# Attention values: one eviction into a plain buffer and four DMAs onto the block diagonal, in place of four evictions

## The reference

```
x = _ln(transpose(msa, (0, 3, 2, 1)), ln_m_g, ln_m_b)      # 256 columns of 32 tokens of 64
q = heads(x @ Wq);  k = heads(x @ Wk);  v = heads(x @ Wv)  # 8 heads of 8
g = sigmoid(heads(x @ Wg + bg))
scores = einsum('blhnd,blhmd->blhnm', q, k) / sqrt_c + bias
w = softmax(scores, axis=-1)
attn = g * einsum('blhnm,blhmd->blhnd', w, v)
out = attn @ Wo + bo
...
logits = x @ router_w + router_b                           # 2048 tokens, 8 experts, the best 2 each
h = silu(gate) * up
y = einsum('te,etd->td', weights, expert_out)
```

## Time and profile before

| what | us |
|---|---|
| median of 3 runs | 355.83 |
| the runs | 355.47 to 358.65 |
| the profiled execution, its own time | 359.83 |
| its span in the trace | 358.0 |
| busy in the span: TensorE | 295.7 (83%) |
| VectorE | 276.0 (77%) |
| ScalarE | 209.9 (59%) |
| GpSimd | 202.7 (57%) |

### The profile page before, as it was taken

One profiled execution on the slowest core, in us unless ns is written; L12 is line 12 of the kernel. 1 busy time (PEld: TensorE's weight loads), 2 busy tenths in 40 slices (PEclk: granted clock), 3 DMA queues, 4 the chain that ended last, 5 costly groups with the idle time before them and its releaser, 6 DMA issues.

```text
span 358.0 us, 11098 instructions
## 1 busy us (share of the span) xinstructions
PE 295.7 (83%) x3773; PEld 178.3 (50%) x3774; DVE 276.0 (77%) x569; ACT 209.9 (59%) x380; POOL 202.7 (57%) x176
## 2 busy tenths in 40 slices
PE   0596868878878755977989989999999999899970
PEld 0186435545545532322446556666666666566640
DVE  3998785989999996778658767888888878688750
ACT  0277688989999964277135435555555555455520
POOL 2833132786889889452233476575756575565451
PEclk9998975989999997885599999999999999999995
DMA  7450100355544457679126777977768687767942
GB/s 183 84 180 3 61 2 6 117 187 171 185 168 142 152 168 226 234 221 240 37 53 112 114 124 123 134 127 125 132 119 134 116 149 109 128 120 131 116 63 30
DMA packets 70656, 45.00 MB, mean 126 GB/s; under 512 B 47992, under 2 KB 63608, under 8 KB 70240
## 3 DMA queue, kind: packets, MB, share of 16 engines
q1 hardware_dynamic: 62368, 34.09, 37.4%
q0 software_dynamic: 7488, 10.39, 20.3%
q10 hardware_dynamic: 768, 0.14, 0.3%
HBM read 23.43 MB, written 9.63 MB: 92 GB/s over the span
## 4 chain that ended last, share of the span: by engine, by line
PE 41%; DVE 16%; DMA 13%; issue 11%; ACT 9%; POOL 4%; POOLq 2%; ACTq 0%; DVEq 0%
PE bank L862 15%; DMA out_dram<-w_stage,gate 8%; PE bank L885 7%; DMA w_stage<-token_rows,gate 4%; ACT kq L1040 3%; PE bank L679 3%; DVE maxes L1327 3%; PE bank L762 2%; PE bank L588 2%; PE bank L850 2%; PE bank L670 2%; DVE s_exp L1336 2%; POOLq L527 2%; PE bank L552 2%; DMA w_exp<-in_L_conv_pairs_dram 1%
## 5 line engine op out<-in xcount | busy, mean ns | idle before, releaser
L862 PE MATMUL bank<-w_exp,v_t 128*128 x468 | 113.6, 379 | 2.0 <-DVE v_t L1526 1.4
L534 POOL DMA_INDIRECT out_dram<-w_stage,gate x39 | 62.2, 1594 | 54.4 <-DMA out_dram<-w_stage,gate 32.5
L862 PEld LDWEIGHTS bank<-w_exp,v_t 128*128 128x128 f16 x468 | 45.9, 98 | 42.2 <-issue 4.2
L885 PE MATMUL bank<-w_exp,kq 128*128 x468 | 57.9, 273 | 1.0 <-DVE w_stage L1572 0.8
L520 POOL DMA_INDIRECT w_stage<-token_rows,gate x39 | 40.1, 1029 | 27.9 <-ACT gate L1131 11.2
L1152 ACT ACTIVATE kq<-w_stage 128x512 f16<-128x512 f32 x38 | 23.9, 630 | 53.8 <-DVE w_stage L1555 53.8
L885 PEld LDWEIGHTS bank<-w_exp,kq 128*128 128x128 f16 x468 | 45.6, 98 | 15.0 <-issue 1.1
L438 POOL TENSOR_TENSOR w_exp<-w_stage,w_exp 128x1024 f16<-128x1024 f32 x16 | 34.1, 2134 | 12.3 <-ACT w_exp L1051 12.3
L1562 DVE TENSOR_TENSOR kq<-w_stage,kq 128x512 f16<-128x512 f32 x38 | 26.3, 693 | 16.7 <-ACT kq L1152 16.7
L1547 DVE TENSOR_TENSOR kq<-bank,v_t 128x512 f32<-128x512 f32 x39 | 26.9, 691 | 11.4 <-PE bank L862 11.3
L1555 DVE TENSOR_TENSOR w_stage<-s_exp,kq 128x512 f32<-128x512 f32 x39 | 27.1, 694 | 3.9 <-DVE kq L1547 0.4
(11 more groups left out here) (255 smaller groups left out, 519.2 us busy)
## 6 DMA issues: line engine op xcount, KB each, us to landing
w_stage<-in_L_ffn_gate_w_dram SPq DMA_DIRECT2D x8, 512.0 KB, 3.6
w_stage<-in_L_ffn_up_w_dram SPq DMA_DIRECT2D x8, 512.0 KB, 3.4
w_stage<-in_L_ffn_down_w_dram SPq DMA_DIRECT2D x8, 512.0 KB, 3.6
x_rows<-in_x_dram SPq DMA_DIRECT2D x8, 256.0 KB, 5.9
out_dram<-x_rows SPq DMA_DIRECT2D x4, 512.0 KB, 6.1
v_t<-in_L_ffn_up_b_dram SPq DMA_DIRECT2D x2, 1024.0 KB, 10.6
token_rows<-z_stack SPq DMA_DIRECT2D x4, 512.0 KB, 6.4
z_two<-z_stack SPq DMA_DIRECT2D x6, 256.0 KB, 2.4
```

Of the source, the lines that this page charges most:

```text
L534: pool.indirect_dma_start(out, bass.IndirectOffsetOnAxis(t_scatter[:, b:b + 1], 0), yw[b % 2], None, compute_op=ALU.add).then_inc(s[f"y_la ...
L862: mm = pe.matmul(GU[par][k][:], xs[par][:, c, :], w_exp[:, w * W_EXP + k * W_PIECE + c * FF:][:, bass.ds(e, FF)], start=(n == 0), stop=(n ...
L885: mm = pe.matmul(YB[:, 0:L_COL], hs[par][:, c, :], w_exp[:, w * W_EXP + 2 * W_PIECE + c * L_COL:][:, bass.ds(e, L_COL)], start=(n == 0), s ...
```

## The change

`values_out` becomes one ScalarE instruction on all 128 partitions, into a new plain buffer `v_row`, with its columns turned so that the eight channels stand outside and the 64 (tile, head) places inside. A new function `place_values` issues four DMAs from ScalarE's own queue, one for each group of 32 partitions, which copy `v_row` to the block of that group: 32 rows of 2 KB each, 64 KB a DMA, 256 KB a pair. Its place in ScalarE's order is behind the tanh. The layout of `v_t` changes with it, so that each row of such a DMA is one contiguous piece; the matmul of `attend` then reads its 36 columns with a step of 64 elements. The semaphore `v_ready` is split: `v_copied` (one each pair) releases `project`, `v_in` (64 each pair) releases `attend` and the next eviction into `v_row`. The wait for the attention of two pairs before (`av_ps`) and that for the zeros and ones go from the eviction to the DMAs. The 16 KB of gate biases, which had a buffer of their own, now lie in `v_row`, and SyncE loads them only when the values of all pairs have been placed.

```diff
+        v_row = sb("v_row", [P, TOK])
+        gate_rows = v_row[0:EXPERTS, :]
...
+        v_tile = [v_t[:, i, :].rearrange("p (b c t) -> p b c t", b=GROUP, c=VCOL) for i in range(2)]
...
-            sp.dma_start(gate_rows[:], gate_b).then_inc(s["rows_in"], 16)
...
+            sp.wait_ge(s["v_in"], 16 * GROUP * PAIRS)
+            sp.dma_start(gate_rows, gate_b).then_inc(s["rows_in"], 16)
...
-                    pe.wait_ge(s["v_ready"], GROUP * j)
+                    pe.wait_ge(s["v_copied"], j)
...
-                    pe.wait_ge(s["v_ready"], GROUP * (j + 1))
+                    pe.wait_ge(s["v_in"], 16 * GROUP * (j + 1))
...
-                                       v_tile[par][:, 4 * c + q, h, :, :], start=True, stop=True)
+                                       v_tile[par][:, :, :, HEADS * (4 * c + q) + h], start=True, stop=True)
...
             def values_out(j):
                 act.wait_ge(s["v_ps"], j + 1)
+                if j >= 1:
+                    act.wait_ge(s["v_in"], 16 * GROUP * j)
+                act.activation(v_row[:].rearrange("p (c t) -> p c t", c=D_HEAD),
+                               bank[4].rearrange("p (t c) -> p c t", c=D_HEAD), ACT.Copy).then_inc(s["v_copied"], 1)
+
+            def place_values(j):
                 if j == 0:
                     act.wait_ge(s["ones_ready"], N_ONES)
                 if j >= 2:
                     act.wait_ge(s["av_ps"], 2 * (j - 1))
+                act.wait_ge(s["v_copied"], j + 1)
                 for u in range(GROUP):
                     rows = slice(32 * u, 32 * u + 32)
-                    act.activation(v_tile[j % 2][rows, :, :, u, 0:D_HEAD],
-                                   bank[4][rows, :].rearrange("p (t h c) -> p t h c", t=8, h=HEADS),
-                                   ACT.Copy).then_inc(s["v_ready"], 1)
+                    act.dma_start(v_tile[j % 2][rows, u, 0:D_HEAD, :],
+                                  v_row[rows, :].rearrange("p (c t) -> p c t", c=D_HEAD)).then_inc(s["v_in"], 16)
...
                     values_out(j + 1)
                     gate_tanh(j + 1)
+                    place_values(j + 1)
                 weights_high(j, 1)
...
             values_out(0)
             gate_tanh(0)
+            place_values(0)
```

More of the change, by code:

```diff
@@ L94, in build @@
         small_i = sb("small_i", [P, 2], i32)
-        gate_rows = sb("gate_rows", [EXPERTS, FF])
+        v_row = sb("v_row", [P, TOK])
+        gate_rows = v_row[0:EXPERTS, :]
         maxes = sb("maxes", [P, 2, 2 * CHUNK])
@@ L144, in build @@
         g_col, b_col, bo_col, bg_col, qb_col, kb_col, vb_col, gb_col = (small[:, 144 + i:145 + i] for i in range(8))
-        v_tile = [v_t[:, i, :].rearrange("p (t h b c) -> p t h b c", t=8, h=HEADS, b=GROUP) for i in range(2)]
+        v_tile = [v_t[:, i, :].rearrange("p (b c t) -> p b c t", b=GROUP, c=VCOL) for i in range(2)]
         N_TABLES = 13
@@ L251, in build @@
             q_ps k_ps v_ps g_ps s_ps av_ps at_ps wo_ps
-            q_ready k_ready max_ready sub_ready exp_ready et_ready v_ready
+            q_ready k_ready max_ready sub_ready exp_ready et_ready v_copied v_in
             rden_ready norm_ready gate_ready gate_one gated_ready x1_ready w_hi_done w_hi_pool w_lo_done
@@ L401, in _ @@
                 for u in range(4):
-                    ones(pool.memset(t[32 * u:32 * u + 32, :, :, u, D_HEAD], 1.0))
+                    ones(pool.memset(t[32 * u:32 * u + 32, u, D_HEAD, :], 1.0))
             pool.wait_ge(s["pair_v"], 1)
@@ L808, in gate_bias_rows @@
                         pe.wait_ge(s["gb_ready"], e - 4)
-                    pe.matmul(bank[GATE_BANK[e]], ident[0:EXPERTS, e:e + 1].broadcast_to([EXPERTS, P]), gate_rows[:],
+                    pe.matmul(bank[GATE_BANK[e]], ident[0:EXPERTS, e:e + 1].broadcast_to([EXPERTS, P]), gate_rows,
                               start=True, stop=True).then_inc(s["gb_ps"], 1)
```

## The result

The changed kernel takes 361.93 us at the median of 4 runs (360.73 to 365.89), the kernel before 357.24 in the runs beside it: a ratio of 1.0146, 95 % interval 1.0088 to 1.0203. A later comparison gave 1.0129 (1.0078 to 1.0179). So the change makes the kernel slower, by some 5 us, where the forecast said 2.5. The profiled execution took 362.11 us, its span 360.3.

What follows compares the result with a forecast made beforehand. Two near-equal loops, VectorE's 10.24 us and ScalarE's queue, were taken to bound settled pairs. Way in -0.5, interval 1 +1.25 and intervals 3 to 6 +1.75 gave +2.5 on 355.83: 358.3 us, 8-in-10 range 353.5 to 362.

Steps and rivals of the forecast that it cites:

- the price of the four issues: ScalarE's queue, each pair: four DMA issues take 1.96 us together, bounds 1.6 and 2.6.
- way in: Pair 0, before the settled loop: values end 1.94 us sooner, issues partly covered by the tanh; about -0.5 us.
- interval 1: Keys to keys: tanh already waits for TensorE, so nothing is won and issues delay the keys; +1.25 us.
- interval 2: Keys to keys: ScalarE's 1.23 us idle before the queries absorbs the added issue time; 0.
- intervals 3 to 6: Four settled pairs, keys to keys: 10.85 us each on ScalarE's loop, 43.4 instead of 41.66; +1.75 us.
- the rival of dear issues: ScalarE's four issues cost 2.2 to 2.6 us beside the weight loads; total 359.5 to 361.5 us; chance 0.17.
- the three rows: Measured issue prices: four in a row at kernel start 1.96 us, a single SyncE issue 0.37, tiny ScalarE-queue ones 0.62.
- Where the issues stand: ScalarE's queue: issues start with the tanh, not in the gap ahead; the weight conversion waits for the fourth.
- The evictions: ScalarE: one 128-partition eviction of 0.645 us replaces four of 2.58 a pair; about 1.0 of 1.94 removed is won.
- Values too late: Rival at the attention's start: landing beyond 4.5 us costs some 5 us per us, 362 to 368; chance 0.09.
- slower attention: Rival on TensorE: strided reads lengthen attention from 0.77 us, unseen to 1.7, 365 at 3; chance 0.06 with a clock drop.
- VectorE's gaps: VectorE, settled pairs: gaps of about 0.6 us a pair ahead of the row maxima.

Runs made afterwards that it cites:

- the second two: Second profiles of both kernels, each rerun unchanged: the kernel before 358.79 us, 0.9973; the changed kernel 363.37 us, 1.0129.
- eight-issue kernel: Changed kernel with the same bytes placed by eight DMAs of 16 partitions on ScalarE's queue instead of four of 32: 388.03 us in one run.
- the kernel with SyncE's issues: Changed kernel with the same four placement DMAs issued from SyncE's queue instead of ScalarE's: 355.49 us, 0.9955 of the kernel before.
- The split kernel: Changed kernel with two of the four issues ahead of the tanh and two behind it, still on ScalarE's queue: 355.57 us, 0.9916 of the kernel before.
- layout-only kernel: Changed kernel without placement DMAs: four evictions of 32 partitions straight into the new layout, gate biases still loaded late: 354.55 us, 0.9874 of the kernel before.
- late biases: Kernel before with only SyncE's gate-bias load moved behind the attention's last weight load: 357.86 us, 0.9951.
- repeated matmuls: Kernel before with half of the attention's matmuls issued twice, 96 instead of 64: 359.40 us, 1.0071.

## Why the prediction was wrong

The direction and the mechanism were right, the size was half of what came. The step that failed is the price of the four issues, taken as 1.96 us from the four at the kernel's start.

| part | forecast | the first two profiles | the second two |
|---|---|---|---|
| way in, keys of pair 0 to pair 1 | -0.5 | -1.20 (16.58 to 15.38) | -1.22 |
| interval 1 | +1.25 | +0.79 | +0.40 |
| interval 2 | 0 | +1.79 | +0.92 |
| intervals 3 to 6 | +1.75 | +4.73 | +5.26 |
| to the last keys | +2.5 | +6.11 | +5.36 |

- **The price.** 2.44 to 2.72 in pairs 1 to 6, above the upper bound of 2.6 in five of the six; the rival of dear issues, with a chance of 0.17, is what came. The prediction's own sum holds with it: issues of 2.59, the mean of pairs 3 to 6, in place of 1.96 make the pair 11.48 and intervals 3 to 6 longer by 4 x 11.48 - 41.66 = 4.26, of 4.73 measured; its 5 us for each us of issue make the whole 2.5 + 5 x 0.63 = 5.7, against 6.11 and 5.36. The prediction named the three rows and both ends; the mistake was to take the middle one as nearest, because it had the same queue and partitions. The eight-issue kernel shows that partitions don't set the price (611 ns for 16, 612 for 32); the kernel with SyncE's issues shows that the queue doesn't either (2.43 for four). Nor would a nearer row have helped. The copy of z_two is a copy within SBUF in mid-attention, and SyncE's timeline of the kernel before shows its issue, the same in all four pairs that have one:

```profile
73.12 0.47 SPq L305 DMA_DIRECT2D z_two<-z_stack  x1
```

  By it the four would have been 4 x 0.47 + 0.1 = 2.0, no better than 1.96. Nearest in size were the tiny DMAs on ScalarE's queue, 0.62, which the prediction kept as a bound only. Right behind four placements, in the kernel with SyncE's issues, the same z_two issue took 0.59. What in a DMA or in its queue sets the price stays open.
- **Where the issues stand.** They began within 0.1 of the tanh in every pair but the first, as said: an instruction that still waits holds those behind it. The split kernel shows it from the other side. The rule of the Trainium skill, "DMA: Bandwidth & Descriptors", section "Issuing engines are not separate DMA queues", that another issuing engine saves only usually small sequencer time, describes what happened here, but not its size: 2.4 us a pair moved to SyncE were worth 1.9 % of the kernel (1.0146 to 0.9955).
- **The evictions.** 0.60 for the turned one, 0.645 assumed. Right.
- **The tanh** starts at 119.53, 3.46 behind the scores (116.07); 3.45 was said. From conversion to keys 2.48, said 2.46. Right.
- **Way in.** The part I didn't take happened: the sequencer got ahead of the table load, by two issues.
- **Interval 2.** The 1.23 of idle time that should have absorbed the issues was not there. TensorE's timeline of the changed kernel:

```profile
68.33 1.05 PE L681 MATMUL bank<-kq 32*32 32x128 f32 x63
70.43 1.43 PE L681 MATMUL bank<-kq 32*32 32x128 f32 x65 [1.06 <-issue]
```

  It stands still for 1.06 in the middle of the scores, with nothing that the trace shows as the reason, so that the tanh waits 3.30. In the kernel before, a like stop of 2.11 (ahead of 75.79) fell into the second attention half, where only the queries waited. The second profile of the changed kernel has half as much here, and the kernels without issues behind the tanh also took more than the 11.93 of before: 12.17 (layout only) and 12.72 (SyncE's issues). How such a stop falls is not in any step of mine.
- **Values too late** and **slower attention**: the attention grew to 1.22, within the 1.7 that the prediction called unseen, and the layout-only kernel bears that out. The rule of the Trainium skill, "SBUF — State Buffer", section "Door 1: The DMA port swizzle (why `[64,N]` ≈ `[32,N]`)", that each access that crosses to a new 16 B line pays, is agreed with in direction (0.77 to 1.22 with a step of 256 B), and yet it cost nothing: the layout-only kernel's settled pairs are 10.23 to 10.28. Values landed 3.4 us behind their issue at the median, 4.5 being the limit; one attention in a settled pair waited 0.83 for them and delayed the scores by 0.12 (92.64 against keys that ended at 89.73 + 2.79 = 92.52).
- **VectorE's gaps** were forecast at 0.6 a pair, ahead of the row maxima; in the settled pairs they stand ahead of the transposes (0.93 and 0.61), which wait for ScalarE's exponentials. Place and sum were wrong: 1.54 a pair, where the kernel before has 0.47.
- **What no step had.** The layout alone gains 1.3 % (0.9874 and 0.9862), so what the DMAs put on top of it is the larger: 1.0146 / 0.9874 = 1.028, some 10 us. Set against the layout-only profile, the parts of the table's first profiles are -1.05, +2.31, +1.55 and +5.36, together +8.17. That the whole was off by only some 2 us is therefore partly luck: a gain that the prediction didn't have hid part of a loss that it had too small.
- **Where the layout's 4.5 us lie** can be said only in part, by the layout-only profile and the second one of the kernel before. The first interval is 1.5 (11.75 to 10.24 at a higher clock; more matmuls ahead of the attention give the same). Another 1.5 lies at the end of the stage: from the last keys to the last residual row 27.29 against 25.76. But the kernels with late biases and with repeated matmuls have the old layout and 25.70 and 25.71 there, so this is not shown to be the layout's. Some 1.2 lie ahead of the attention: the keys of pair 0 begin at 38.16 instead of 39.40, and at 36.52 to 38.71 in all nine profiles of the new layout, against 37.91 to 39.83 in the five of the old. The prediction gave the ones in plain rows 0, "long before use". But in both kernels GpSimd's setting of them stands on the chain that ended last, and took 0.49 less; GpSimd's timeline before and in the layout-only kernel:

```profile
14.37 2.04 POOL L402 MEMSET v_t<- 32x64 f32 x8
```

```profile
14.23 1.55 POOL L403 MEMSET v_t<- 32x64 f32 x8
```

  No run changes it alone, so what it is worth is not shown. The rest, and why the clock is higher in the kernels of the new layout, stays open. That the attention takes longer is not enough, as the kernel with repeated matmuls shows.

The two medians differ by 4.7, less than the 6.11, and the spans of the two profiles by only 2.3 (358.0 to 360.3): in the changed kernel's, the keys of pair 0 begin 1.39 earlier (36.52 against 37.91) and the end of the stage is shorter (25.97, against 28.55 and 27.29 in the two profiles of the kernel before). The profiled execution of the kernel before was 4 us above the median of its own runs, and part of that lay there.

## What to carry to other kernels

A DMA issue has a price on the engine that issues it, some 0.6 us for the copy here, whether it moved 16, 32 or 64 rows (0.37 and 0.47 for two other DMAs). Count issues, not bytes, and put them on a queue that nobody waits for, or ahead of an instruction that waits anyway, not between it and work that others wait for. Busy time doesn't show them: read the idle time that ends in "issue". When a change bundles two edits, run each alone: here a gain of 1.3 % in the layout was hidden under a loss of nearly 3 % in the issues.

## What the runs showed of the hardware

- An issue of 16, 32 or 64 partitions of 2 KB rows within SBUF took 611, 612 and 571 ns at the median on ScalarE's queue, 590 on SyncE's; on SyncE's queue a weight load from DRAM took 370, the 256 KB copy of z_two 470.
- Issues ran beside a running ScalarE instruction (119.59 beside the tanh from 119.53) and beside a table load (44.57 beside 44.51), but not past a tanh that waited (1.21 in that pair).
- Reading 36 columns with a step of 256 B, the 64 small matmuls of an attention half took 1.22 us, in steps of one element 0.77.
- Five useless matmuls ahead of a stretch moved its granted clock from 0.71 to 0.93 and made it 1.56 us shorter, in a kernel whose TensorE is not the busiest engine there (9.54 of 11.75, ScalarE 10.21).
- GpSimd set 32 x 64 ones in 203 ns in steps and in 144 ns in plain rows; a ScalarE eviction of 32 x 512 took 638 ns into the old layout and 588 into the new one (medians).
